# Probabilities turned by VectorE blocks and SBUF transfers in place of TensorE transposes

## The reference

```
q, k, v = layernorm(x) @ wq.T + bq, ctx @ wk.T + bk, ctx @ wv.T + bv     # 16 heads of 32
scores  = q k / sqrt(32), masked                                          # 256 x 256 per head
x       = x + softmax(scores) v @ wo.T + bo
probs   = softmax(layernorm(x) @ w_gate)          # 8 experts, the best 2 of each token
x       = x + sum over the 2 of  weight * (silu(a) * g) @ c_proj[e],   a, g = layernorm(x) @ c_fc[e]
```

## Time and profile before

| | |
|---|---|
| time, median of 3 runs | 3031.32 us (3030.25 to 3031.86) |
| profiled execution | 3035.1 us, span 3033.3 us |
| attention block | until about 1420 us of the span |
| TensorE (PE) busy | 2938.5 us, 97% |
| VectorE (DVE) busy | 1533.9 us, 51% |
| ScalarE (ACT) busy | 1542.7 us, 51% |
| GpSimd (POOL) busy | 1262.6 us, 42% |
| mean granted TensorE clock | 0.984 |

### The profile page before, as it was taken

One profiled execution on the slowest core, in us unless ns is written; L12 is line 12 of the kernel. 1 busy time (PEld: TensorE's weight loads), 2 busy tenths in 40 slices (PEclk: granted clock), 3 DMA queues, 4 the chain that ended last, 5 costly groups with the idle time before them and its releaser, 6 DMA issues.

```text
span 3033.3 us, 55379 instructions
## 1 busy us (share of the span) xinstructions
PE 2938.5 (97%) x17824; PEld 2489.2 (82%) x17824; DVE 1533.9 (51%) x5034; ACT 1542.7 (51%) x3910; POOL 1262.6 (42%) x1911
## 2 busy tenths in 40 slices
PE   6999999999999999994999999999999999999998
PEld 6888888888888888883788888888888888888886
DVE  5777777777777777773433223333242332423331
ACT  4777777777777777772323223233232322322321
POOL 4566666666666666664112122222212121222211
PEclk8999999999999999996999999999999999999999
DMA  5444444444444444432534343344434443444322
GB/s 162 124 126 132 124 122 127 126 132 124 124 126 125 133 125 124 125 104 83 135 87 101 77 98 78 90 88 91 86 94 88 94 94 77 98 80 94 68 44 28
DMA packets 290390, 315.35 MB, mean 104 GB/s; under 512 B 46528, under 2 KB 234944, under 8 KB 288576
## 3 DMA queue, kind: packets, MB, share of 16 engines
q1 hardware_dynamic: 227040, 178.48, 22.5%
q0 software_dynamic: 32768, 67.26, 12.8%
q10 hardware_dynamic: 30304, 66.07, 6.7%
HBM read 109.53 MB, written 67.90 MB: 58 GB/s over the span
## 4 chain that ended last, share of the span: by engine, by line
PE 51%; DMA 1%; SPq 0%; issue 0%; POOL 0%; DVE 0%; ACT 0%; POOLq 0%
PE a_ps L1219 17%; PE g_ps L1219 17%; PE y_ps L1234 17%; DMA out<-y,recs 0%; SPq L1012 0%; DMA xg<-xn_rows,gather_ids 0%; POOL xg L1058 0%; DMA lists<-table 0%; DMA x_quarters<-xg 0%; DVE xe_lo L1153 0%; POOL out L1086 0%; ACT xe_hi L1113 0%; DVE x_turned L1166 0%; ACT y L1146 0%; DVE act_part L1166 0%
## 5 line engine op out<-in xcount | busy, mean ns | idle before, releaser
L1086 POOL DMA_INDIRECT out<-y,recs x128 | 207.2, 1618 | 1185.7 <-ACT y L1146 751.8
L373 POOL TENSOR_SCALAR probs<-probs,row_inv 128x256 f32<-128x256 f32 x1024 | 492.3, 493 | 417.0 <-DVE row_inv L586 412.6
L577 DVE CUSTOM_DVE_ANT_0 probs<-scores_ps,mask_add,row_any 128x256 f32<-128x256 f32 x1024 | 454.6, 480 | 272.2 <-PE scores_ps L793 269.3
L1193 DVE TENSOR_TENSOR hidden<-act_part,g_ps 128x512 f32<-128x512 f32 x192 | 132.1, 688 | 860.0 <-ACT act_part L1132 860.0
L477 ACT ACTIVATE probs<-probs,low 128x256 f32<-128x256 f32 x1024 | 513.7, 504 | 99.9 <-DVE low L577 85.9
L462 ACT COPY probs_t<-probs_t_ps 128x512 f32<-128x512 f32 x512 | 299.9, 586 | 193.9 <-PE probs_t_ps L805 145.0
L1219 PE MATMUL a_ps<-xe_hi,fc_hi 128*128 128x512 f32 x768 | 300.3, 391 | 39.7 <-DVE xe_lo L1153 39.4
L805 PE MATMUL probs_t_ps<-ident,probs 128*128 128x128 f32 x2048 | 310.8, 274 | 7.5 <-POOL probs L373 7.5
L1219 PE MATMUL a_ps<-xe_lo,fc_hi 128*128 128x512 f32 x768 | 299.6, 390 | 0.0
L1219 PE MATMUL a_ps<-xe_hi,fc_lo 128*128 128x512 f32 x768 | 299.5, 390 | 0.0
L1219 PE MATMUL g_ps<-xe_lo,fc_hi 128*128 128x512 f32 x768 | 298.8, 389 | 0.0
(11 more groups left out here) (170 smaller groups left out, 6656.1 us busy)
## 6 DMA issues: line engine op xcount, KB each, us to landing
k_stack<-qk_hi SPq DMA_DIRECT2D x512, 64.0 KB, 2.0
q_stack<-qk_hi SPq DMA_DIRECT2D x512, 64.0 KB, 2.8
x_quarters<-xg SPq DMA_DIRECT2D x512, 64.0 KB, 2.0
fc_raw<-in_c_fc SPq DMA_DIRECT2D x24, 1024.0 KB, 5.8
k_stack<-qk_lo SPq DMA_DIRECT2D x256, 64.0 KB, 2.0
q_stack<-qk_lo SPq DMA_DIRECT2D x256, 64.0 KB, 2.9
out<-x_xn ACTq DMA_DIRECT2D x32, 512.0 KB, 3.3
xn_rows<-x_xn ACTq DMA_DIRECT2D x32, 512.0 KB, 3.6
```

Of the source, the lines that this page charges most:

```text
L373: last = nc.gpsimd.tensor_scalar(probs[:, r, t, :], probs[:, r, t, :], row_inv[:, r, t:t + 1], 1.0, ALU.mult, ALU.mult)
L577: last = nc.vector.tensor_tensor_reduce(out=probs[:, s % 4, t, :], in0=scores_ps[s % 2][:, t, :], in1=mask_add[:, t, :], scale=row_any[:, ...
L1086: nc.gpsimd.indirect_dma_start(out=out[:, :], out_offset=bass.IndirectOffsetOnAxis(ap=recs[:, i * CT + t, 0:1].bitcast(U32), axis=0), in_= ...
L1193: nc.vector.tensor_tensor(hidden[:, m % 2, :], act_part[:, m % 2, :], g_ps[m % 2][:, :], ALU.mult).then_inc(gated, 1)
```

## The change

All of it is in attention_block. The slots of one head become chunks of four heads (c = 0 to 3), and the order of each engine is written anew by chunks; routing of element n-2 now lies in step n, so there is one more step (STEPS).

- Queries and keys stay in fp32: no split, no stacks, no stacking transfers. ScalarE writes both (qk_out). The scores of four heads are made at once (score), each head on its own 32 rows of TensorE, into four PSUM banks.
- The probabilities are not transposed on TensorE. VectorE turns each head in 32x32 blocks into `blocks` (turn), and SP moves the blocks between partition groups into `probs_t` (move): 16 transfers per chunk, each of 32 partitions x 2 KB. `blocks` and `probs_t` have two places each, `probs` a ring of eight heads.
- The LayerNorms are applied by ScalarE (normalise), for which GpSimd computes an offset besides the root.
- The gate takes its weights, padded to 32 columns, as the stationary operand on four column groups (gate); ScalarE copies the parts, and two small matmuls add them (gate_sum).

```diff
-        probs_t_ps = [ps(f"probs_t_ps{i}", [P, TILES, SEQ]) for i in range(2)]
+        scores_ps = [ps(f"scores_ps{r}", [P, TILES, SEQ]) for r in range(HPC)]
...
+                def move(g):
+                    if g == 1:
+                        sp.wait_ge(w_split, 4)
+                    need(sp, attended, g - 1)
+                    settle(sp)
+                    sp.wait_ge(turned, (g + 1) * HPC)
+                    for j in range(GROUPS):
+                        for a in range(GROUPS):
+                            sp.dma_start(probs_t[a * DK:(a + 1) * DK, g % 2, j, :],
+                                         blocks[j * DK:(j + 1) * DK, g % 2, a, :]).then_inc(moved[g % 2], 16)
...
+                    nc.gpsimd.tensor_scalar(minus_mean[:, which, :], moments[:, which, :, 0], -1.0, 0.0,
+                                            ALU.mult, ALU.add).then_inc(chain, 1)
...
+                    nc.gpsimd.tensor_tensor(offset[:, which, :], minus_mean[:, which, :], rstd[:, which, :],
+                                            ALU.mult).then_inc(rstd_done, 1)
...
+                        if has(n):
+                            for r in range(3):
+                                scale(g + r)
+                        if c == 0 and has(n + 1) and n >= 0:
+                            root(0, n + 1, ln1_var, ln1_chain, ln1_rstd, xn_ready)
+                        if c == 2 and has(n - 1):
+                            root(1, n - 1, ln2_var, ln2_chain, ln2_rstd, xn2_ready)
+                        if has(n):
+                            scale(g + 3)
...
+                def turn(g):
+                    group, r = divmod(g, HPC)
+                    dve.wait_ge(normed, g + 1)
+                    if r == 0:
+                        need(dve, moved[group % 2], QUARTERED * (group // 2))
+                    head = TILES * TILES * DK
+                    nc.vector.transpose(
+                        blocks[:, group % 2, :, r * head:(r + 1) * head].rearrange("p a (b l) -> p b a l", l=DK),
+                        probs[:, g % RING, :, :].rearrange("p t (u a l) -> p (t u) a l", a=GROUPS, l=DK)).then_inc(
+                            turned, 1)
...
+                    for c in range(DC):
+                        g = n * HEADS + c * HPC
+                        attn = tail if c < 2 else heads
+                        if c == 2 and proj and n >= 0:
+                            x_lo(n + 1, 1)
+                        if c == 2 and tail:
+                            x2_out(n - 1, 0)
+                        if c != 2 and attn:
+                            attn_lo(n * DC + c - 2)
+                        if heads:
+                            mask_scores(g)
+                            mask_scores(g + 1)
+                            invert(g)
+                            mask_scores(g + 2)
+                            invert(g + 1)
+                            mask_scores(g + 3)
+                        if c == 0 and late:
+                            logits_out(n - 2)
+                        if c == 2 and late:
+                            place_out(n - 2)
+                        if heads:
+                            turn(g)
+                        if c == 1 and proj and n >= 0:
+                            x_lo(n + 1, 0)
+                        if c == 2 and tail:
+                            x2_out(n - 1, 1)
+                        if heads:
+                            invert(g + 2)
+                        if c == 2 and attn:
+                            attn_lo(n * DC + c - 2)
+                        if c == 2 and tail:
+                            moments_x2(n - 1)
+                        if heads:
+                            turn(g + 1)
+                        if c == 0 and proj and n >= 0:
+                            moments_x(n + 1)
+                        if c == 1 and late:
+                            route(n - 2)
+                        if heads:
+                            invert(g + 3)
+                            turn(g + 2)
+                        if c == 3 and late:
+                            record(n - 2)
+                        if heads:
+                            turn(g + 3)
...
+                def attend(g):
+                    b, c = divmod(g, DC)
+                    pe.wait_ge(moved[g % 2], QUARTERED * (g // 2 + 1))
+                    need(pe, at_split, g)
...
+                def score(g):
+                    b, c = divmod(g, DC)
+                    pe.wait_ge(q_ready, g + 1)
+                    pe.wait_ge(k_ready, g + 1)
+                    need(pe, masked, g * HPC)
+                    for t in range(TILES):
+                        for r in range(HPC):
+                            rows_of = slice(r * DK, (r + 1) * DK)
+                            last = nc.tensor.matmul(scores_ps[r][:, t, :], qk[rows_of, b % 2, 0, c, t * P:(t + 1) * P],
+                                                    qk[rows_of, b % 2, 1, c, :], start=True, stop=True)
+                    last.then_inc(scored, 1)
```

1064 lines of the change are left out of this document (554 added, 510 removed).

## The result

The kernel after takes 3333.86 us (median of 4 runs, 3327.88 to 3340.48) against 3030.78 us for the kernel before on the same chip: a ratio of 1.100, interval 1.098 to 1.102. The change makes the kernel 303 us slower. The forecast was 3155 us with a cheap issue (0.38 us) on SP's queue; rival A, with 0.64 us, gave 3353 us. So the time lies outside the forecast's own range of 3080 to 3240 us. The profiled execution of the kernel after takes 3334.2 us, its span 3332.4 us.

The account below looks back on a forecast made before the run. TensorE was taken to bound the kernel before (41.7 us per element); after, VectorE's order 42.0 + late moves 1.8 + clock 1.4 = 45.2 us. Over 32 elements +112, plus 8 for the last step: 3155 us, range 3080 to 3240.

Parts of the forecast that it names:

- rival A: SP's queue in attention: 0.64 us per issue for the moves too, period 51.4 us, 3353 us; chance 0.24.
- What bounds the kernel before: Attention half: TensorE, busy 400.00 of 400 us, sets the 41.69 us period per batch element; other engines have slack.
- TensorE's work after: Attention half, per element: 11.3 us removed, 7.2 for fp32 scores and 0.7 for the gate added, 38.3 us left.
- The turns: VectorE in attention: sixteen block transposes per element, 711 ns each, 0.65 with overlap, 10.4 us; at most twice that.
- VectorE's table: VectorE's order over an element's four chunks: 10.6, 9.8, 12.2 and 9.4 us, sum 42.0, with 6 us of it waiting.
- wait of the fourth turn for the root: Chunks 0 and 2: GpSimd computes the LayerNorm root, 1.9 us, before scaling the fourth head, so VectorE's last turn waits.
- What the transfers add: SP's moves in attention: 16 issues at 0.38 us, 6.1 us, make chunk 0's masks 1.8 us late; period 43.8 us.
- What the clock adds: TensorE's attention and scores behind a wait run at 1.2 GHz: 1.4 us counted, ends 0 and 4, period 45.2 us.
- The last step: The extra step ending attention: the last element's gate, routing and records run alone, adding 8 us.
- B: TensorE's scores: row groups don't overlap, 47.1 us of work, period 48 to 51 us, about 3290 us; chance 0.07.
- C: Faster: VectorE's order fits better and moves land in time, period 39.2 us, about 2960 us; chance 0.19.
- D: SP's issues overlap with landings, no scores late, only VectorE's 42.0 us remains, about 3050 us; chance 0.05.

Follow-up runs that it names:

- The gate alone: The kernel before with only the new gate (weights stationary on four column groups, parts added by two small matmuls): 3015.50 us, ratio 0.993 to 0.996.
- 4 transfers: The kernel after with only 4 of a chunk's 16 transfers, the other turned probabilities left out (layer not computed): 3141.15 us.
- 12 and 8 transfers: Against the kernel after: 12, four diagonal blocks copied by ScalarE behind the next chunk's exponents, 3251.51 us; 8 of 16, the rest left out, 3155.49 us.
- the same four copies early or late: Kernel after, ScalarE copying the four blocks that keep their partitions, SP issuing 12: ahead of next chunk's exponents 3428.56 us, behind them 3251.51 us.

## Why the prediction was wrong, step by step

- **What bounds the kernel before: right.** The gate alone shows it: of 0.8 us taken from TensorE 0.52 come off the period.
- **TensorE's work after: right in kind.** A score group takes 1.07 us, the lower end (1.0, 1.8 taken), so the row groups and the loads overlap. The gate and its sums take about 0.9 us (0.7 taken). It no longer mattered, as TensorE waits.
- **The turns: right.** 703 ns at the median (711 taken), so the output's order costs nothing more.
- **VectorE's table: right in its sum.** 41.3 us on average against 42.0, and 40.9 with 4 transfers. But with 4 transfers the period is 45.0 us, because 4.2 us pass ahead of chunk 0, for which the table has no term. Moving the root takes 3.6 us of this away and 2.6 us of period with it, and leaves the sum of the chunks where it was (41.4). The table's wait of the fourth turn for the root is real, but without it the time goes into the wait for the exponents.
- **What the transfers add: the step that failed.** The term was 16 x 0.38 = 6.1 us; measured 10.1 to 11.2 us, 0.66 us an issue. The mechanism (move, attend, score, mask on a loop; VectorE late ahead of chunks 0, 1 and 3) is what the trace shows, and with 0.64 us rival A had the period within 0.4 us. That it came so close is in part luck: it counts nothing for the clock, 1.8 us for scores that take 1.07 at the full clock and 1.87 behind a wait, and nothing for the late masks of chunk 0 that have another cause. My mistake was to choose between two rows by the form of the transfer, when the stack transfers shared route, size and partition count with the new ones and only the runs differed. The kernels with 12 and 8 transfers hold SP about 8 and 5.3 us per move and have periods of 48.5 and 45.7 us; the forecast's 6.1 us would lie between, by interpolation near 46.5 us (an estimate), where 45.2 was forecast. So the rest of the sum was short by about 1.3 us, and the price of the issue made the other 4.5. The small rest is luck too: in the kernel with 8 transfers no mask is late by a move, and the 4.2 us ahead of chunk 0 stand where the forecast had 1.8 for the move and 1.4 for the clock.

  The Trainium skill, DMA: Bandwidth & Descriptors, Issuing engines are not separate DMA queues, calls the time that it takes the sequencer to initiate a DMA "usually small relative to the DMA itself". The trace does not agree: an issue of 0.59 us stands against 2.0 us to landing, and 16 in a row, 10.6 us, against one landing. The number of issues decides, and halving the bytes did nothing.
- **What the clock adds: the mechanism right, its size not settled.** Score groups behind a long wait take 1.87 us instead of 1.07. Raising the clock to 0.97 gave back 0.35 us of period where 1.4 was counted, with part of the groups still slow.
- **The last step: right in size, wrong in place.** 9.7 us outside the stores' intervals (8 taken), most of it ahead of the first store.
- **Rivals.** B (row groups one after the other) is out by the 1.07 us. C is out: the moves are late, and even with 4 transfers the period was 45.0 us. D is out: landings overlap with issues, but the issues come one after the other. A is the result, with the luck told above.

## What to carry to other kernels

Before a step that TensorE does is given to transfers, multiply the number of issues by the price of the same route (here 0.66 us with both sides in SBUF) and put the product on the loop it belongs to; sixteen small transfers took 11.6 to 12.7 us from the first issue to the attention that waits for them, and half the bytes changed nothing. A wait that is visible beside a stronger bound is worth nothing until that bound goes: the same exchange of root and scaling gave 0 and then 88 us. Even then, look at where the time went: the wait that the exchange was made for only changed its name, and the gain came from another. And copies or issues lent to another engine cost their wait and what stands behind it in that engine's order, not only their own length: the same four copies early or late differ by 177 us.

## What the runs showed of the hardware

- One issue on SP's queue, back to back, one run per partition: 589 to 606 ns with both sides in SBUF, for 16 to 128 partitions and up to 256 KB, and 421 to 432 ns with HBM on one side (ScalarE's queue 612 and 453). Four runs per partition on 128 partitions, in SBUF: 665 ns. Alone, with a wait ahead of it, 507 and 358 ns. SP and ScalarE issue side by side at 594 and 614 ns, as they do alone.
- Four fp32 score groups on four row groups, 16 records of 256 columns with loads of 128 columns each, take 1.07 us in all.
- ScalarE's copy of 32 partitions x 512 columns takes 0.62 us, as much as one of 128 partitions (0.58).
- Beside GpSimd's scatters of the records, instructions of two other engines began late, both at the same time and some microseconds after TensorE's work that they needed (scores done by 1061.6 us, gate by 1062.2). In the kernel after, ScalarE, VectorE and GpSimd:

```profile
1065.54 0.37 ACT L519 COPY gate_parts<-bank_a 128x256 f32<-128x256 f32 x1 [4.24 <-remote]
```
```profile
1065.59 0.48 DVE L623 CUSTOM_DVE_ANT_0 probs<-scores_ps,mask_add,row_any 128x256 f32<-128x256 f32 x1 [3.77 <-remote]
```
```profile
1063.43 0.97 POOL L335 DMA_INDIRECT table<-rec,place_i  x1 [0.30 <-issue]
```

With 4 transfers and the scatters elsewhere these waits are gone (ScalarE's 82.8 us of 1100 ahead of the gate copy became 27.2, put down to TensorE). They also went when only the root was moved and the scatters stayed, so it takes more than the scatters; that it is the meeting of the two in time is my reading, and what passes between the engines there is not settled.
